# Second MLP product of a convolution-attention block: its transfers split over two queues by partition halves, and its moving operand read in another order

## The reference

```python
y = _gelu(y @ fc1_w + fc1_b)                       # 96 -> 192 channels
dw = _gelu(depthwise_5x5(y) + dw_b)
y = y + dw                                         # "s" below
tok2 = y @ fc2_w + fc2_b + tok2                    # 192 -> 96, tok2 is x2
...
x = x + layer0(_gn(x))                             # x1 = x + x2 + s @ fc2_w + fc2_b
x = x + layer1(_gn(x))                             # _gn needs sums and sums of squares of x1
```

## Time and profile before

| | us |
|---|---|
| median of 3 runs | 7700.91 (7690.25 to 7706.97) |
| profiled execution, its own time | 7690.68 |
| its span | 7688.9 |
| stage `fc2` (first x load issued to first work of the next stage) | 5585.0 to 6588.1 = 1003 |

### The profile page before, as it was taken

The page is one execution under the profiler, slowest core; times in us unless marked ns, Lnnn a source line. Parts: engine busy times, 40 slices in busy tenths (PEclk is TensorE's granted clock), DMA queues, the critical chain, the costliest instruction groups (busy, mean ns, idle before and its releaser), DMA issues. The chain is left out here.

```text
span 7688.9 us, 138214 instructions
## 1 busy us (share of the span) xinstructions
PE 6602.4 (86%) x52604; PEld 3232.1 (42%) x52604; DVE 4890.2 (64%) x7370; ACT 3553.5 (46%) x5600; POOL 2457.7 (32%) x3173
## 2 busy tenths in 40 slices
PE   0886999999999999999997898899957768688885
PEld 0332555555555555555553333555500000476662
DVE  6785777777777777777774555788812222454554
ACT  0553666666666666666664666344401101243330
POOL 0443444444444444444445565000012222000000
PEclk9997999999999999999998999999988989787885
DMA  7784333334333434333325886988799999345655
GB/s 300 196 239 124 77 77 78 88 85 91 79 71 73 88 83 92 83 77 77 78 46 155 254 250 206 359 342 344 282 249 274 248 272 250 97 112 140 172 147 164
DMA packets 480460, 1252.80 MB, mean 163 GB/s; under 512 B 159620, under 2 KB 164740, under 8 KB 442628
## 3 DMA queue, kind: packets, MB, share of 16 engines
q1 hardware_dynamic: 444276, 1141.72, 54.3%
q0 software_dynamic: 7168, 50.34, 2.1%
q10 hardware_dynamic: 28368, 51.91, 1.8%
HBM read 731.14 MB, written 458.07 MB: 155 GB/s over the span
## 5 line engine op out<-in xcount | busy, mean ns | idle before, releaser
L727 DVE TENSOR_REDUCE at_mz<-at_ps 128x4 bf16<-128x1024 f32 x1444 | 1774.6, 1229 | 782.5 <-PE at_ps L651 782.2
L600 ACT ACTIVATE at_E<-at_ps 128x1024 f32<-128x1024 f32 x1444 | 1500.9, 1040 | 794.7 <-PE at_ps L663 794.7
L663 PE MATMUL at_ps<-at_qaug,at_k 32*128 32x256 f32 x11552 | 830.0, 401 | 79.2 <-DVE at_qaug L751 79.2
L674 PE MATMUL at_ps<-at_E,at_vaug 128*32 128x256 f32 x11552 | 774.3, 386 | 0.0
L1190 PE MATMUL cv_ps<-cv_yin,cv_band 128*128 128x384 f32 x2304 | 745.4, 486 | 27.9 <-DMA cv_yin<-y_mlp 27.9
L1210 DVE TENSOR_TENSOR cv_yin<-cv_gl,cv_yin 64x384 f32<-64x384 f32 x1152 | 637.5, 553 | 150.8 <-ACT cv_gl L1201 142.9
L663 PEld LDWEIGHTS at_ps<-at_qaug,at_k 32*128 32x128 f32 x11552 | 523.1, 184 | 443.1 <-issue 224.5
L1297 POOL TENSOR_TENSOR f_xa<-f_xa,f_xb 128x3840 f32<-128x3840 f32 (+1 forms) x28 | 213.2, 7636 | 1544.1 <-DMA f_xb<-in_x 1544.1
L540 POOL TENSOR_TENSOR at_share<-at_rden,t_share 128x8 f32<-128x8 f32 x722 | 146.8, 203 | 1558.8 <-DVE at_rden L738 1558.6
L1336 DVE SCALAR_TENSOR_TENSOR f_xa<-f_ps,f_b,f_xa 128x512 f32<-128x512 f32 (+1 forms) x216 | 136.2, 687 | 753.6 <-PE f_ps L1320 753.6
L1317 PE MATMUL f_ps<-f_sa,f_wa 128*32 128x512 f32 (+1 forms) x1728 | 379.8, 958 | 268.2 <-DMA f_sbb<-s_mlp 268.2
(11 more groups left out here) (210 smaller groups left out, 9570.2 us busy)
## 6 DMA issues: line engine op xcount, KB each, us to landing
cv_yin<-y_mlp SPq DMA_DIRECT2D x48, 2340.0 KB, 14.7
s_mlp<-cv_yin SPq DMA_DIRECT2D x48, 2340.0 KB, 8.4
at_rows_in<-y_attention SPq DMA_DIRECT2D x38, 1536.0 KB, 9.4
gn_xin<-in_x SPq DMA_DIRECT2D x16, 3072.0 KB, 23.2
ln_xin<-in_x SPq DMA_DIRECT2D x192, 256.0 KB, 7.6
y_attention<-ln_xin SPq DMA_DIRECT2D x192, 256.0 KB, 3.8
cl_xu<-x SPq DMA_DIRECT2D x128, 384.0 KB, 3.8
cl_xv<-x SPq DMA_DIRECT2D x64, 768.0 KB, 5.5
```

What stands on the lines that cost most here:

```text
L600: act.activation(E[:, m % 2, 2 * p:2 * p + 2, :], psum[:, 2 + 2 * p:4 + 2 * p, :], ACT.Exp).then_inc(exp_done, 1)
L663: i = pe.matmul(psum[:, 2 + h, TOK * j:TOK * j + TOK], k[rows, n % 2, tokens(w, 128 * j, 128)], qaug[rows, m % 2, :], start=True, stop=True)
L674: i = pe.matmul(pv_ps[32 * h:32 * h + VC, 0:TOK], vaug[:, m % 2, z, h, :], E[:, m % 2, h, z * TOK:(z + 1) * TOK], start=(z == 0), stop=(z ...
L727: dve.tensor_reduce(mz[:, m % 2].rearrange("p j (h c) -> p h j c", c=32)[:, 2 * p:2 * p + 2, :, DQ], psum[:, 0:2, :].rearrange("p h (j n) ...
```

## The change

1. **Two queues.** `load_x`, `load_s` and the new `store` take a queue and a half. SP's queue carries the x loads and stores of g = 0, 1 (partitions 0 to 63) and the s loads of rr = 0; ScalarE's queue those of g = 2, 3 (partitions 64 to 127) and of rr = 1. The number, size and pieces of the transfers stay. Stores no longer have ScalarE's queue to themselves: in each queue they stand behind the s loads of the next tile.
2. **Moving operand.** "c b t k q" becomes "c b t q k": the columns of a phase run fastest (8 bytes apart), phases come outside. PSUM then holds a row as 4 phases x 64 columns.
3. **VectorE restores the order.** One instruction for each row (128 x 4 x 64) in place of one for each chunk: PSUM is read in order, `xa` is read and written with 16 bytes from element to element.

```diff
+        def load_x(queue, k, half):
+            ...
+            if k >= 2:
+                queue.wait_ge(stored[k % 2], 16 * XLOADS * (k // 2))
+            for grp in range(CGRP):
+                for rr in range(2):
+                    g = 2 * half + rr
+                    queue.dma_start(xa[32 * g:32 * g + 32, k % 2, grp, 0:count]...,
+                                    group_rows(x2, k, half, rr, grp)).then_inc(xa_loaded[k % 2], 16)
+            if k:
+                queue.wait_ge(xs_done, 2 * k)
+            ...
+        def load_s(queue, v, half):
+            for row, t, at, count in row_sources(v // 2, half, v % 2):
+            ...
+        def store(queue, k, half):
+            queue.wait_ge(x1_done, first[2 * k + 2])
+            queue.wait_ge(squares_done, CGRP * (2 * k + 2))
+            queue.wait_ge(sums_done, 2 * k + 2)
+            ...
         @block.sync
-            load_x(0)
-            load_s(0)
+            load_x(sp, 0, 0)
+            load_s(sp, 0, 0)
+            load_s(sp, 1, 0)
             for k in range(NTILE):
-                load_s(2 * k + 1)
                 if k + 1 < NTILE:
-                    load_x(k + 1)
-                    load_s(2 * k + 2)
+                    load_x(sp, k + 1, 0)
+                    sp.wait_ge(f_done, first[2 * k + 1])
+                    load_s(sp, 2 * k + 2, 0)
+                    sp.wait_ge(f_done, first[2 * k + 2])
+                    load_s(sp, 2 * k + 3, 0)
+                store(sp, k, 0)
 ...
-                    return a[...].rearrange("c q (t k b) -> c b t k q", t=count, b=B)[:, b, :, 0:COLS, :]
+                    return a[...].rearrange("c q (t k b) -> c b t q k", t=count, b=B)[:, b, :, :, 0:COLS]
 ...
                 for grp in range(CGRP):
-                    xc = xa[:, k % 2, grp, b0:b0 + count, jj, :]
-                    pc = psum[:, CGRP * (n % 2) + grp, 0:count * W].rearrange("p (t w) -> p t w", w=W)
-                    i = dve.scalar_tensor_tensor(out=xc, in0=pc, scalar=b2[:, grp:grp + 1], in1=xc, op0=ALU.add, op1=ALU.add)
+                    for row in range(count):
+                        xc = xa[:, k % 2, grp, b0 + row, jj, :].rearrange("p (k q) -> p q k", q=PHASES)
+                        pc = psum[:, CGRP * (n % 2) + grp, row * W:row * W + W].rearrange("p (q k) -> p q k", q=PHASES)
+                        i = dve.scalar_tensor_tensor(out=xc, in0=pc, scalar=b2[:, grp:grp + 1], in1=xc, op0=ALU.add, op1=ALU.add)
 ...
         @block.scalar
+            load_x(act, 0, 1)
+            load_s(act, 0, 1)
+            load_s(act, 1, 1)
+            for k in range(NTILE):
+                if k + 1 < NTILE:
+                    load_x(act, k + 1, 1)
+                    act.wait_ge(f_done, first[2 * k + 1])
+                    load_s(act, 2 * k + 2, 1)
+                squares(2 * k)
+                if k + 1 < NTILE:
+                    act.wait_ge(f_done, first[2 * k + 2])
+                    load_s(act, 2 * k + 3, 1)
+                squares(2 * k + 1)
+                store(act, k, 1)
```

More of the change, by code:

```diff
@@ L1243, in fc2 @@
         s_loads = [sum(4 * len(row_sources(i, rr, 0)) for i in range(k + 1) for rr in range(2)) for k in range(NTILE)]
+        def load_x(queue, k, half):
+            count = tile_rows(k)[2]
+            if k >= 2:
[3 more added lines that the diff above has]
+                    g = 2 * half + rr
+                    queue.dma_start(xa[32 * g:32 * g + 32, k % 2, grp, 0:count].rearrange("c t j w -> c t (j w)"),
+                                    group_rows(x2, k, half, rr, grp)).then_inc(xa_loaded[k % 2], 16)
+            if k:
+                queue.wait_ge(xs_done, 2 * k)
+            for grp in range(CGRP):
+                for rr in range(2):
+                    g = 2 * half + rr
+                    queue.dma_start(xb[32 * g:32 * g + 32, grp, 0:count].rearrange("c t j w -> c t (j w)"),
+                                    group_rows(x, k, half, rr, grp)).then_inc(xb_loaded, 16)
+        def load_s(queue, v, half):
+            for row, t, at, count in row_sources(v // 2, half, v % 2):
+                n = count * PITCH - GAP
+                run = slice(at * PITCH, at * PITCH + n)
+                for f in range(2):
+                    src = sdr[:, f, row, :, t:t + count, :].rearrange("c e t n -> c e (t n)")[:, :, GAP * f:GAP * f + n]
+                    queue.dma_start(sa[:, v % 2, half, 2 * f:2 * f + 2, run], src[0:128]).then_inc(s_loaded[v % 2], 16)
+                    queue.dma_start(sbb[64 * half:64 * half + 64, v % 2, 2 * f:2 * f + 2, run], src[128:MLP]).then_inc(s_loaded[v % 2], 16)
+        def store(queue, k, half):
+            count = tile_rows(k)[2]
+            queue.wait_ge(x1_done, first[2 * k + 2])
+            queue.wait_ge(squares_done, CGRP * (2 * k + 2))
+            queue.wait_ge(sums_done, 2 * k + 2)
+            for grp in range(CGRP):
+                for rr in range(2):
+                    g = 2 * half + rr
+                    queue.dma_start(group_rows(x1, k, half, rr, grp),
+                                    xa[32 * g:32 * g + 32, k % 2, grp, 0:count].rearrange("c t j w -> c t (j w)")).then_inc(stored[k % 2], 16)
         @block.sync
@@ L1251, in _ @@
                 sp.dma_start(b2[32 * g:32 * g + 32, :], p["fc2_b"].rearrange("(s c) -> c s", s=CGRP), allow_slow_non_contiguous=True).then_inc(w_loaded, 16)
[L1253 to L1278, removed]
@@ L1288, in _ @@
+            for u in range(2):
+                sp.wait_ge(stored[u], 16 * XLOADS * (NTILE // 2))
         @block.gpsimd
@@ L1306, in lines @@
                 def lines(a, b):
-                    return a[:, :, b0 * PITCH:b0 * PITCH + count * PITCH].rearrange("c q (t k b) -> c b t k q", t=count, b=B)[:, b, :, 0:COLS, :]
+                    return a[:, :, b0 * PITCH:b0 * PITCH + count * PITCH].rearrange("c q (t k b) -> c b t q k", t=count, b=B)[:, b, :, :, 0:COLS]
                 if n == first[v]:
@@ L1346, in _, with squares @@
         def _(act):
-            for v in range(NV):
+            def squares(v):
                 k, jj = v // 2, v % 2
```

## The result

The changed kernel takes 7561.69 us (median of 4 runs, 7560.29 to 7562.95), the kernel before 7695.58 (median of 4, 7675.86 to 7706.97). The ratio is 0.9821 with a 95% interval of 0.9801 to 0.984: 134 us faster, where 241 were forecast. The profiled execution of the changed kernel took 7560.29 us, its span is 7558.5.

What follows compares the result with a forecast made beforehand. The stage was taken as bound by transfers, at 253 GB/s. Terms 252 + 318 + 126 + 42 + 3 + 21 = 762 us for 1003, 241 less, gave 7450 profiled and 7460 us as median; range 7390 to 7640.

Steps and rivals of the forecast that it cites:

- start and tail: Ends of the stage: 3 us at the start and 21 us after the last s landing.
- Part 1: x loads in the stage: 100.7 MB over two queues at 400 GB/s, between bounds 223 and 409, taking 252 us.
- Rival A: x and s loads: two load streams still meet at times, x 300 and s 280 GB/s, time 7590; chance 0.15.
- Rival B: Loads: engines stay in step on one half, second queue brings nothing, time 7742, or 7781 without any gain; chance 0.12.
- Part 2: s loads in the stage: 101.9 MB at 320 GB/s, between bounds 232 and 400, taking 318 us.
- Rival D: s loads uncontended too, at 400 GB/s: stage 699, time 7397; no chance of its own, lower edge of the forecast's 0.65.
- Part 3: Stores, now queued behind s loads: 50.3 MB at about 400 GB/s, 126 us in full on the path.
- Part 4: Gaps before x loads that wait for a tile's stores: 12 holes of 3.5 us, 42 us.
- Part 5: TensorE: eight instructions near 0.95 us instead of 1.88, busy time from 729 to about 370 us, wholly beside the transfers.
- Part 6: VectorE and ScalarE: 0.479 us an instruction, at worst doubled, still under the transfers; ScalarE's waits drain no queue; cost nothing.

Runs made afterwards that it cites:

- e3: Changed kernel with x loads given to the queues by row group, so both queues write the same half of the partitions at a time: 7667.14 us, ratio 0.9958.
- e9: Changed kernel with ScalarE's x transfers writing to a buffer in HBM instead of partitions 64 to 127: 7505.43 us in one run, before 7679.09.
- e2: Kernel before with only the new moving operand and VectorE's new instructions, still one queue for loads and ScalarE's for stores: 7618.12 us, ratio 0.9889.
- e5: Changed kernel with the 128-partition part of s also split into two 64-partition transfers, one half per queue: 7477.73 us, ratio 0.9714.
- e4: Changed kernel with a tile's stores ahead of the last s loads in both queues, and on ScalarE both halves' squares ahead of them: 7551.77 us, ratio 0.9802.
- e1: Changed kernel with the old moving operand and VectorE's old instructions, leaving only the two queues of the change: 7600.42 us, ratio 0.9869.
- e8: Changed kernel with ScalarE's x loads copying a block of SBUF instead of reading HBM: 7649.27 us in one run, before 7679.09.

## Why the prediction was partly right

The sum had 762 us for the stage; 854 were measured. Term by term, with what the rows give (the x loads are what is left over, and good to some 10 us):

| term | predicted | measured |
|---|---|---|
| x loads | 252 | about 324 |
| s loads | 318 | about 334 |
| stores | 126 | about 126 |
| 12 holes | 42 | 47 |
| start and tail | 24 | about 22 |

**Part 1, the x loads, is the step that failed**, in its size. The direction was right: e3 shows that the halves decide, 220 GB/s against 361. The step "For the lower half's writes nothing differs from the earlier trace rows" took a load beside a store for the model of a load beside a load. e9 is that very case (the other stream writes to HBM) and gives the 406 (400 was forecast); with both streams writing SBUF it is 361 in the row above: 100.7 / 0.361 = 279 us, 27 above the term. The other 45 us come from what that row leaves out: tiles that settle lower, at 340 to 350, the first microseconds after each hole, at 190 to 300 GB/s, and the stage's start, where one queue alone had 204. Rival A, *partial sharing*, named what happened, at 0.15, and its 300 GB/s for x was nearer to the 311 that 100.7 MB in 324 us come to; its 7590 missed by 28 us, the forecast's 7460 by 102. Its case lacked a number, and I had weighed it by one row of another kind of pair.

Rival B, *the halves serialize*, is refuted by the same rows. With it falls, for this kernel, the sentence of the Trainium skill ("SBUF — State Buffer", the section "Can I just issue two DMAs to hit both halves?") that two transfers to the two halves gain 6%: here they took x loads from 223 to 361 GB/s, and at the stage's start from 204, one half alone, to 367. What the page says ahead of it, that each half of the partitions has its own ports, agrees with that start and with e3 for loads. The 223 GB/s that the prediction put beside it are no measure of one half, since that queue alternates between the halves and reached 370 in one tile of e2. One trait of B is there for a while: the slow stretch after each hole looks as if the engines began in step and fell out of it. That is argued from the rates alone.

**Part 2, the s loads**: 320 GB/s was forecast; about 305 came out (101.9 MB in 334 us), 300 in the row above. The reason given, that only the 64-partition piece is split by the change, held: e5 splits the rest and s rises to 342. Rival D, s uncontended at 400, did not come about even there; the ceiling of two load streams is 342 for s and 361 for x.

**Part 3, the stores**: as forecast. Beside each other they run at 400 to 420 GB/s (the first slices of the hole's row above), and the full 126 us are on the path. The split by halves brought them nothing, since they did not have the loads' trouble: in the kernel before, from 6540 to 6545, they ran alone in ScalarE's single queue, 32 partitions a transfer and in the same order of groups as the loads of the earlier trace rows, at

```profile
DMA packets 1091, 2.03 MB, mean 406 GB/s; under 512 B 100, under 2 KB 100, under 8 KB 1091
```

So what is slow is a load into part of the partitions, not a store out of it.

**Part 4, the gaps**: 12 holes as forecast, about 4 us for 3.5. What I missed is that part of their time is given back by s when they are removed (e4: 42 us less idle, 12 us less stage).

**Part 5, TensorE**: 1.05 us for eight instructions where 0.95 was taken, 1.88 the old value. With the products at the lower clock after each idle stretch it comes to 440 us, not 370. It is hidden, as forecast, so the miss costs nothing. The step's cover was right for the changed kernel, but the prediction sold it short as an edit: e1 shows that without it the queues alone leave 54 us more of idle engines, and e2 that alone it is worth 83 us. "It lies beside the transfers" was true of the changed kernel and false of the one before, where s loads waited for TensorE for 99.9 us in all, a row that the prediction did not use. In the sum this did not matter, since a sum made anew from bytes and rates does not contain the old waits.

**Part 6, VectorE**: 0.59 us an instruction in the row above and 0.67 in the mean of all 384, within the 0.48 to 0.96 given; nothing waits for it but the tail. ScalarE's place between the loads cost nothing either: SP's stores waited 82.8 us for the squares, but the queues were draining s loads meanwhile, and all 12 holes stand behind the stores, none ahead of them.

**Outside the stage** the sum had nothing, and the profile lost 19 us there (5.5 ahead of the stage, 13 behind). The same unchanged code behind the stage varied between 1086 and 1127 us over all runs. The four executions of the changed kernel lie within 3 us of each other, so its median carries these 19 us too.

The range, 7390 to 7640, held the time; the likeliest value was 102 us too low. The term of x is 72 of that and s 16; the 19 lost outside the stage come on top, and the 10 that the forecast had added between the profiled execution and the median go off, since here the two were 1.4 apart. That the range held owes something to its width: it ran from rival D to beyond rival A. (One reading was off and changed no term: the earlier trace rows have 21 us from the start of the last products to the next stage and 19 from their end, not 22.)

## What to carry to other kernels

Loads that write at most half of the partitions at a time are worth splitting over two queues so that the two always write different halves (partitions 0 to 63 and 64 to 127): here it took them from 223 to about 350 GB/s, and a second queue on the same half brought nothing. A load over all 128 partitions beside them is worth splitting in the same way: it took 58 us off the stage, and only then was the order of stores and loads worth its 31 us. Stores gained nothing from the halves. To price two streams of loads, look for a row with two streams of loads: a load beside a store is a faster pair.

## What the runs showed that was not expected

- Two load streams into different halves stop at about 350 GB/s (340 to 366 for x, 342 for s); one alone into one half has 204; a load stream beside one that writes to HBM reaches 406 (e9).
- Stores of 32 partitions each run at 406 GB/s alone in one queue, loads of the same shape and order at 223.
- After each hole loads run at 190 to 300 GB/s for some microseconds before they reach 361, with every engine busy all the while.
- The rate of a single queue of 32-partition loads isn't one number: 223, 261, and in two tiles of e2 315 to 370 GB/s, with the same transfers in the same order.
- Copies within SBUF in pieces of 8 and 10 KB took two thirds of the engines' time for 2.78 MB in 16 us (e8): 174 GB/s for 66.5% of them, so some 270 if they had them all, below the 409 of the earlier trace rows.
- The moving operand's order decides TensorE's pace: eight instructions of 512 columns in 1.88 us with 2600 bytes from element to element, 1.05 with 8. The old pace was the same at a granted clock of 0.50 and of 1.00; the new one is 1.87 at 0.50 and 1.05 at 1.00.
